# Graph-kernel layer with LayerNorm: one stationary operand moved, the banks of the preparation emptied by other engines, and three lists reordered

## The chip, the cores and the metric

One core of a Trainium2 chip runs the whole kernel. The metric is device time in microseconds, the median of several executions. The engines are called as in the profile: PE (TensorE), DVE (VectorE), ACT (ScalarE), POOL (GpSimd) and SP (SyncE, which here only issues DMAs).

## The reference, cut to what matters

`x` is 32 x 256 x 512, `adj` a 256 x 256 mask of zeros and ones. All is float32.

```python
z_l = einsum('bnd,ed->bne', x, W_lang);  z_g = einsum('bnd,ed->bne', x, W_grav)
v   = einsum('bnd,ed->bne', x, W_V)
zn  = z_l / max(norm(z_l), EPS)
A_l = max(zn zn^T, 0) * not_eye
d2  = max(sq + sq^T - 2 z_g z_g^T, 0)          # sq = row sums of z_g^2
A_g = exp(-d2 / (2 sigma^2)) * not_eye
K_l = A_l*adj / max(rowsum(A_l*adj), EPS);  K_g = the same of A_g
K   = w_l K_l + (1 - w_l) K_g                  # w_l = sigmoid(gate_logit)
x   = layernorm(x + (K v) W_O^T)
```

## The kernel before

**Products.** Every float32 matrix that PE multiplies is kept as two fp32r parts, hi (ACT rounds a bank or a tile into it) and lo (DVE subtracts hi from the source), and a product of two matrices is a sum of part products, hi·hi, hi·lo and lo·hi. The weights are first folded: M_g = W_g^T W_g for g = L (lang) and G (grav), so that x M x^T gives both Gram matrices, and WVO = W_V^T W_O^T. M is symmetric. What is computed for x is P = M x^T and then X = x P, of which X plus its own transpose is the Gram matrix. `m_hi` and `m_lo` are the parts of M, `md_hi` is the diagonal blocks of M with their lower triangle halved and joined with lo, and `wvo_hi`, `wvo_lo` the parts of WVO.

**The loop.** The 32 samples go in 16 pairs. The list of PE for pair p, with q = p - 1, is: eight projections `project(p, k)`, k = 0 to 7 (j = k mod 4 is the block of 128 output features, g = k div 4 is L or G), each into one bank of 128x512; `value(0, 0)` (12 products); four tiles of X, `x_tile` (8 products each); `value(0, 1)`; two tiles K times v of the sample 0 of pair q, `k_times_v` (6 products each); `value(1, 0)`; `value(1, 1)`; two tiles K times v of sample 1. Each product has a stationary operand of 128x128 and a moving one of 128x512. A projection has four products with x hi and four with x lo, one for each block i of 128 input features. That is 64 + 48 + 32 + 24 = 168 products a pair.

**Banks.** Banks 0 to 3 are used in turn by the preparation units, the projections and the values: a projection k waits until DVE has made the lo part of projection k - 4 (`proj_ready`). Banks 4 and 5 hold X, 6 and 7 K times v. ACT turns a projection's bank into `p_hi`, then DVE makes `p_lo`; the X tiles need all eight of them.

**Other engines.** Per pair DVE also transposes x blocks (`turn`), makes `hT_lo` (`turn_lo`), transposes X as it comes back from HBM (`turn_x`), adds (`gram`), masks, sums, scales (`gauss_masked`, `inverse_masked`, `cosine_masked`, `row_factors`, `kernel_sum`), transposes K (`turn_k`), splits it (`kt_lo_part`), and adds x (`residual`). `inverse_masked` needs the row of inverse norms in all partitions: `store_r` writes it to HBM and `spread_r` brings it back into `r_row`. X and K are rearranged through HBM as well (`spill_x` and `return_x`, `spill_k` and `return_k`). `load_x` brings x for the residual into `x_nat`, and `store` writes the output. All of these DMAs are issued by SP, in one list by hand. Every engine's list is written out by hand as the function `pair`, with semaphore waits between engines; there is no scheduler. Pairs 0, 1, 14 and 15 are unrolled, pairs 2 to 13 are a loop over two. The last pair has its own list on each engine, in which X and K are turned by PE.

**Preparation.** 22 units u = 0 to 21 go through banks u mod 4: UPPER L 0 to 3, UPPER G 0, then MIRROR L 1, WO_TURN 0, UPPER G 1, MIRROR L 2, WO_TURN 1, UPPER G 2, MIRROR L 3, WO_TURN 2 and 3, UPPER G 3, and MIRROR G 1, WVO 0, MIRROR G 2, WVO 1, MIRROR G 3, WVO 2, WVO 3. UPPER g i makes a block row of M_g from its diagonal block on (12 products of 512, 384, 256 or 128 columns), MIRROR copies the blocks below the diagonal by transposes of `m_hi`, WO_TURN transposes W_O, WVO makes a block row of WVO (12 products of 512). `m_lo` is corrected by the ratio of the diagonals: `diagonals` collects these, `scales` makes four small factors and `scaled_rest` passes over four slices of `m_lo`; then POOL makes `md_hi` of them (`join_triangles`, semaphore `m_ready`). DVE empties the MIRROR banks, POOL makes both parts of W_V.

## Time and profile before

| | us |
|---|---|
| median of 3 runs | 666.3 (665.96 to 666.48) |
| the profiled execution, device time | 666.75 |
| its span in the trace | 665.0 |
| PE busy | 650.5 (98%) |
| DVE busy | 538.7 (81%) |
| ACT busy | 376.6 (57%) |
| POOL busy | 138.8 (21%) |

The trace covers one execution; 1.75 us of its device time lie outside the span. Times below count from the span's start. A PE product is listed with its full latency of 389 ns, but products follow one another at a shorter distance; the distance is read from the starts. PEclk is the granted clock, 1.00 being 2.4 GHz. A duration of DVE or ACT in a list is some 0.08 us longer than the distance to the next operation behind it.

### The profile page before, as it was taken

How to read it: one execution, taken by the hardware profiler on the slowest of the kernel's cores; microseconds unless marked ns; L12 is line 12 of the kernel's file. 1: busy time of each engine (PE TensorE's matmuls, PEld its weight loads, DVE VectorE, ACT ScalarE, POOL GpSimd, SP SyncE). 2: the span in 40 equal slices, each digit the busy share in tenths (PEclk: the TensorE clock that was granted, in tenths of full speed). 3: DMA queues.
4: the chain of work that ended last, by engine and by line, in shares of the span. 5: the costliest groups of instructions: out<-in, count | busy, mean ns of one | idle time of the engine just before them, and what ended most of it. 6: DMA issues, size and time to landing. Idle time of an engine off the chain costs nothing.

```text
span 665.0 us, 10795 instructions
## 1 busy us (share of the span) xinstructions
PE 650.5 (98%) x2892; PEld 538.4 (81%) x2892; DVE 538.7 (81%) x1438; ACT 376.6 (57%) x697; POOL 138.8 (21%) x292
## 2 busy tenths in 40 slices
PE   8799999999999999999999999999999999999995
PEld 7688888888888888888888888888888888888784
DVE  6974878888788888888888798878888888887886
ACT  4242544665557465665656466555746566563746
POOL 4620202130311112131221213031111213121123
PEclk9799999999999999999999999999999999999999
DMA  9120627456483847658483765748384665647423
GB/s 300 33 83 13 190 66 231 118 185 164 149 231 116 235 107 225 137 159 205 151 231 88 235 147 173 174 143 235 110 235 112 212 147 161 175 147 221 156 79 126
DMA packets 141509, 106.48 MB, mean 160 GB/s; under 512 B 40112, under 2 KB 115632, under 8 KB 141488
## 3 DMA queue, kind: packets, MB, share of 16 engines
q1 hardware_dynamic: 140768, 104.40, 55.8%
q0 software_dynamic: 288, 1.05, 0.5%
q10 hardware_dynamic: 432, 0.79, 0.3%
q8 instruction: 9, 0.15, 0.1%
q14 instruction: 12, 0.10, 0.1%
HBM read 65.80 MB, written 40.40 MB: 160 GB/s over the span
## 4 chain that ended last, share of the span: by engine, by line
PE 92%; DVE 4%; DMA 1%; ACT 1%; issue 0%; SPq 0%; POOL 0%; POOLq 0%; DVEq 0%; ACTq 0%
PE bank L1370 57%; PE bank L1435 16%; PE bank L1439 16%; PE bank L1392 1%; DMA x_nat<-in_x 1%; DVE m_lo L968 1%; DVE x_nat L947 1%; DMA xs<-in_L_gnn_W_lang 0%; PE bank L1402 0%; DVE p_lo L1016 0%; DVE work L1071 0%; PE bank L1478 0%; DVE m_lo L935 0%; DVE work L1105 0%; ACT y L778 0%
## 5 line engine op out<-in xcount | busy, mean ns | idle before, releaser
L1439 PE MATMUL bank<-hT_lo,m_hi 128*128 128x512 f32 x512 | 136.8, 389 | 0.0
L718 ACT ACTIVATE p_hi<-bank,m_scale 128x512 fp32r<-128x512 f32 x128 | 87.6, 686 | 74.3 <-PE bank L1439 73.3
L1439 PEld LDWEIGHTS bank<-hT_lo,m_hi 128*128 128x128 f32 x512 | 96.1, 188 | 20.0
L1016 DVE SCALAR_TENSOR_TENSOR p_lo<-bank,m_scale,p_hi 128x512 fp32r<-128x512 f32 x128 | 92.7, 742 | 17.8 <-ACT p_hi L718 17.5
L722 ACT CAST v_hi<-bank 128x512 fp32r<-128x512 f32 x60 | 34.9, 581 | 118.7 <-PE bank L1370 118.6
L1370 PE MATMUL bank<-p_hi,hT_hi 128*128 128x512 f32 x256 | 99.7, 389 | 0.6 <-DVE p_lo L1016 0.6
L1370 PE MATMUL bank<-wvo_hi,hT_hi 128*128 128x512 f32 x256 | 99.9, 390 | 0.0
L1370 PE MATMUL bank<-wvo_lo,hT_hi 128*128 128x512 f32 x256 | 99.6, 389 | 0.0
L1370 PE MATMUL bank<-wvo_hi,hT_lo 128*128 128x512 f32 x256 | 99.6, 389 | 0.0
L1370 PE MATMUL bank<-p_lo,hT_hi 128*128 128x512 f32 x256 | 99.6, 389 | 0.0
L1154 DVE SCALAR_TENSOR_TENSOR y<-bank,x_nat 128x512 f32<-128x512 f32 x60 | 40.3, 688 | 37.7 <-DMA x_nat<-in_x 22.4
L598 POOL TENSOR_TENSOR rnorm<-norm,minus_half 128x2 f32<-128x2 f32 x32 | 35.2, 1101 | 135.0 <-DVE norm L1041 135.0
L733 ACT COPY xs<-bank 128x512 f32<-128x512 f32 x64 | 37.4, 584 | 42.7 <-PE bank L1370 42.6
L1435 PE MATMUL bank<-hT_hi,m_lo 128*128 128x512 f32 x192 | 59.2, 390 | 0.3 <-DVE p_lo L1016 0.3
L1435 PE MATMUL bank<-hT_hi,m_hi 128*128 128x512 f32 x192 | 59.1, 389 | 0.0
L1370 PEld LDWEIGHTS bank<-p_hi,hT_hi 128*128 128x128 f32 x256 | 48.1, 188 | 11.0 <-DVE p_lo L1016 1.0
L1370 PEld LDWEIGHTS bank<-wvo_hi,hT_hi 128*128 128x128 f32 x256 | 48.1, 188 | 10.2 <-DVE p_lo L1016 0.3
L1370 PEld LDWEIGHTS bank<-wvo_hi,hT_lo 128*128 128x128 f32 x256 | 48.0, 188 | 10.0
L1370 PEld LDWEIGHTS bank<-p_lo,hT_hi 128*128 128x128 f32 x256 | 48.0, 188 | 9.9
L1370 PEld LDWEIGHTS bank<-wvo_lo,hT_hi 128*128 128x128 f32 x256 | 48.1, 188 | 9.9
L1435 PE MATMUL bank<-hT_hi,md_hi 128*128 128x512 f32 x128 | 49.8, 389 | 0.0
L623 POOL TENSOR_TENSOR msq<-row_sq,one_by_d 128x2 f32<-128x2 f32 x30 | 5.9, 198 | 197.8 <-ACT junk_a L770 197.7
(155 smaller groups left out, 1250.6 us busy)
## 6 DMA issues: line engine op xcount, KB each, us to landing
x_blk<-in_x SPq DMA_DIRECT2D x128, 128.0 KB, 3.3
x_spill<-xs SPq DMA_DIRECT2D x30, 512.0 KB, 2.9
xq<-x_spill SPq DMA_DIRECT2D x120, 128.0 KB, 3.1
x_nat<-in_x SPq DMA_DIRECT2D x30, 512.0 KB, 4.6
out_y<-y SPq DMA_DIRECT2D x30, 512.0 KB, 3.3
k_spill<-work SPq DMA_DIRECT2D x30, 256.0 KB, 2.2
...
```

The costliest lines, as they stand in the source:

```text
L598: nc.gpsimd.tensor_tensor(rnorm[:, b, 0:NT], norm2[:, b], minus_half[:], ALU.pow).then_inc(pool_steps, 1)
L718: nc.scalar.activation(p_hi[:, :, j, g, :], src[:].rearrange("p (b n) -> p b n", b=2), ACT.Copy, scale=m_scale[:, g, j:j + 1]).then_inc(pr ...
L722: nc.scalar.copy(last_v(m_hi, b, t) if is_last(p) else v_hi[:, b, t], src[:]).then_inc(proj_hi, 1)
L733: nc.scalar.copy(dst, src).then_inc(x_saved, 1)
L947: nc.vector.tensor_tensor_reduce(out=x_nat[:, g, s, a:e], in0=tile[:, g, i, a:e].bitcast(F32), in1=ident[:], scale=sign, scalar=0.0, op0=A ...
L968: nc.vector.scalar_tensor_tensor(out=m_lo[:, g, i, i * P:], in0=m_hi[:, g, i, i * P:].bitcast(F32), scalar=steps_of[g][:, 4, i:i + 1], in1 ...
L1016: nc.vector.scalar_tensor_tensor(out=p_lo[:, :, j, g, :], in0=src[:].rearrange("p (b n) -> p b n", b=2), scalar=m_scale[:, g, j:j + 1], in ...
L1154: nc.vector.scalar_tensor_tensor(out=y[:, b, t], in0=kv_bank[t][:], scalar=1.0, in1=x_nat[:, b, t], op0=ALU.mult, op1=ALU.add, accum_out=r ...
L1370: last = pe.matmul(dst, lhsT, rhs, start=(n == 0), stop=(n == len(steps) - 1))
L1392: last = pe.matmul(dst[:, cols], lhsT, rhs, start=(n == 0), stop=(n == len(steps) - 1))
L1435: pe.matmul(pbank(k)[:], stationary, hi[i], start=(i == 0), stop=False)
L1439: last = pe.matmul(pbank(k)[:], m_hi[:, g, i, c], lo[i], start=False, stop=(i == DT - 1))
```

## The change

The lo part of the first 128 features of x (i = 0) is no longer a moving operand in the projections with j > 0. In its place each X tile gets a ninth product, with that lo part stationary and `p_hi` of block 0 moving. The lo products of the projections with j = 0 stay, with `md_hi` for the diagonal block. A pair has 58 + 48 + 36 + 24 = 166 products.

```diff
-                for i in range(DT):
-                    last = pe.matmul(pbank(k)[:], m_hi[:, g, i, c], lo[i], start=False, stop=(i == DT - 1))
+                for i in range(1 if j > 0 else 0, DT):
+                    last = pe.matmul(pbank(k)[:], md_hi[:, g, 0] if i == 0 else m_hi[:, g, i, c], lo[i], start=False,
+                                     stop=(i == DT - 1))
...
                     steps += [(lhsT, part[:, b, i].rearrange("p g n -> p (g n)")) for part in (p_hi, p_lo)]
+                steps.append((hT_lo[parity][:, 0, b, t * P:(t + 1) * P], p_hi[:, b, 0].rearrange("p g n -> p (g n)")))
```

On PE the fourth to the sixth row below are projection k = 1 of a pair (bank3), L1439 and L1464 being the products with x lo.

```order
L1439 MATMUL bank2<-hT_lo0,m_hi 128x512 x4
L1435 MATMUL bank3<-hT_hi0,m_lo 128x512
L1435 MATMUL bank3<-hT_hi0,md_hi 128x512
L1435 MATMUL bank3<-hT_hi0,m_hi 128x512 x2
L1439 MATMUL bank3<-hT_lo0,m_hi 128x512 x4
```

```order
L1464 MATMUL bank2<-hT_lo0,m_hi 128x512 x3
L1459 MATMUL bank3<-hT_hi0,m_lo 128x512
L1459 MATMUL bank3<-hT_hi0,md_hi 128x512
L1459 MATMUL bank3<-hT_hi0,m_hi 128x512 x2
L1464 MATMUL bank3<-hT_lo0,m_hi 128x512 x3
```

The upper piece is before, the lower one after: the last row has lost one product, as it has in the six projections with j > 0.

**Preparation.** ACT, not DVE, empties the MIRROR banks, in the order of the units, and a new function says which semaphore frees a bank. ACT also makes the hi part of W_V, POOL only the lo part. The first half of `join_triangles` no longer waits for `scaled_rest`. The wait of DVE for `m_ready` moves from ahead of pair 0 to its first `diagonal`.

```diff
+            def value_weight_hi(k):
+                act.wait_ge(w_loaded[2][k // 2], 16)
+                nc.scalar.copy(by_feature(w_parts[2][0][:, k]), in_order(raw[2][:, k])).then_inc(v_hi_ready, 1)
...
+                act.wait_ge(prep_done, u + 1)
                 if kind == MIRROR:
-                    return
-                act.wait_ge(prep_done, u + 1)
+                    nc.scalar.copy(m_hi[:, g, i, 0:i * P], src[:, 0:i * P]).then_inc(mirrored, 1)
+                    return
...
+            def emptied(u):
+                if prep_units[u][0] == MIRROR:
+                    pe.wait_ge(mirrored, mirrors_upto(u))
+                else:
+                    pe.wait_ge(prep_lo, upto_unit(u))
...
-                    pe.wait_ge(prep_lo, u - 3)
+                    emptied(u - 4)
...
-                if kind == UPPER and g == L:
-                    diagonals(L, i)
-                    if i == DT - 1:
-                        scales(L)
-                        scaled_rest(L)
-                if kind == UPPER and g == G and i < DT - 1:
-                    diagonals(G, i)
+                if kind == UPPER and (g, i) != (G, DT - 1):
+                    diagonals(g, i)
                 if u in SPLIT_AT:
                     turn_lo(0, 0, SPLIT_AT[u])
-                if u in TURN_AT:
-                    turn(0, TURN_AT[u])
-                if (kind, g, i) == (MIRROR, G, 1):
+                if (kind, g, i) == (UPPER, G, DT - 1):
+                    turn(0, 0)
                     diagonals(G, DT - 1)
+                    scales(L)
+                    scaled_rest(L)
+                if (kind, i) == (WVO, 0):
+                    turn(0, 1)
+                if (kind, i) == (WVO, 1):
                     scales(G)
-                if (kind, g, i) == (WVO, None, 1):
+                if (kind, i) == (WVO, 2):
                     scaled_rest(G)
```

On DVE, behind the diagonals of UPPER L 3, before. L957 to L963 are `scales(L)`, L968 is `scaled_rest(L)`, L935 empties the bank of UPPER G 0.

```order
L957 TENSOR_SCALAR junk_d<-junk_d 128x4
L959 RECIPROCAL junk_d<-junk_d 128x4
L961 TENSOR_TENSOR junk_d<-junk_d 128x4
L963 TENSOR_SCALAR m_scale<-junk_d 128x4
L968 SCALAR_TENSOR_TENSOR m_lo<-m_hi,junk_d,m_lo 128x512
L968 SCALAR_TENSOR_TENSOR m_lo<-m_hi,junk_d,m_lo 128x384
L968 SCALAR_TENSOR_TENSOR m_lo<-m_hi,junk_d,m_lo 128x256
L968 SCALAR_TENSOR_TENSOR m_lo<-m_hi,junk_d,m_lo 128x128
L935 TENSOR_TENSOR m_lo<-bank0,m_hi 128x512
```

The same place after. L951 is L935 of before, L955 empties the bank of WO_TURN 0, L963 is `diagonals`.

```order
L951 TENSOR_TENSOR m_lo<-bank0,m_hi 128x512
L963 ISA x_nat,junk_d<-m_hi,ident 128x128
L963 ISA junk_d 128x1
L963 ISA x_nat,junk_d<-m_lo,ident 128x128
L963 ISA junk_d 128x1
L955 TENSOR_TENSOR hT_lo1<-bank2,hT_hi1 128x512
L951 TENSOR_TENSOR m_lo<-bank3,m_hi 128x384
```

The four passes and the four small operations ahead of them have moved 25 rows down, behind UPPER G 3 and the first `turn`.

**Loop.** The lists of DVE, ACT and SP of a pair are reordered; no operation is added or removed there.

```diff
 # DVE
+                gauss_masked(q, 0)
                 gram(q, 0, L)
-                gauss_masked(q, 0)
                 proj_lo_part(p, 0)
                 cosine_masked(q, 0)
                 row_factors(q, 0)
                 proj_lo_part(p, 1)
+                turn_x(q, 1)
                 proj_lo_part(p, 2)
-                turn_x(q, 1)
                 proj_lo_part(p, 3)
-                kernel_sum(q, 0)
                 gram(q, 1, G)
                 proj_lo_part(p, 4)
-                inverse_masked(q, 1)
-                gram(q, 1, L)
+                kernel_sum(q, 0)
                 proj_lo_part(p, 5)
                 proj_lo_part(p, 6)
                 proj_lo_part(p, 7)
+                inverse_masked(q, 1)
                 gauss_masked(q, 1)
+                gram(q, 1, L)
...
+                kt_lo_part(q, 0)
                 turn_r(p, 0)
-                kt_lo_part(q, 0)
                 diagonal(p, 1)
                 turn_lo(p + 1, 1 - parity, 1)
-                residual(q, 0, 0)
                 turn(p + 2, 0)
                 proj_lo_part(p, 8)
                 turn_r(p, 1)
+                residual(q, 0, 0)
                 turn_k(q, 1)
+                residual(q, 0, 1)
+                kt_lo_part(q, 1)
                 proj_lo_part(p, 9)
-                kt_lo_part(q, 1)
-                residual(q, 0, 1)
                 turn_x(p, 0)
                 gram(p, 0, G)
                 residual(q, 1, 0)
+                inverse_masked(p, 0)
                 residual(q, 1, 1)
                 proj_lo_part(p, 10)
-                inverse_masked(p, 0)
                 proj_lo_part(p, 11)
 # SP
                 return_k(q, 0)
+                load_x(q, 0)
+                spill_k(q, 1)
                 store(q - 1, 0)
-                spill_k(q, 1)
-                load_x(q, 0)
+                load_x(q, 1)
                 spill_x(p, 0)
                 return_k(q, 1)
                 store_r(p, 0)
                 return_x(p, 0)
+                store(q - 1, 1)
                 spill_x(p, 1)
-                store(q - 1, 1)
-                load_x(q, 1)
+                store_r(p, 1)
                 spread_r(p, 0)
-                store_r(p, 1)
```

On ACT `squares(q - 1, 0)` goes ahead of the first `proj_hi_part`, `squares(q - 1, 1)` and `gauss(q, 1)` go from behind the eighth to behind the fifth, both `normalise` and `gauss(p, 0)` go a few places ahead, and `save_x(p, 1, 0)` goes behind `kt_hi_part(q, 0)`. The lists of the last pair are as they were.

On DVE, from the x lo split of a pair (L914, L932) to the values, before and then after. L1154 and L1172 are `residual`, L1024 and L1039 the values' lo parts, L1137 and L1155 `turn_k`, L1144 and L1162 `kt_lo_part`.

```order
L1154 SCALAR_TENSOR_TENSOR y,row_sum<-bank6,x_nat 128x512
L906 STREAM_TRANSPOSE hT_raw<-x_blk 128x1024
L1024 TENSOR_TENSOR v_lo<-bank2,v_hi 128x512
L1049 STREAM_TRANSPOSE rnormT<-rnorm 128x32
L1137 STREAM_TRANSPOSE work<-work 128x8x2x32
L1024 TENSOR_TENSOR v_lo<-bank3,v_hi 128x512
L1144 TENSOR_TENSOR kt_lo<-work,kt_hi 128x512
L1154 SCALAR_TENSOR_TENSOR y,row_sum<-bank7,x_nat 128x512
```

```order
L924 STREAM_TRANSPOSE hT_raw<-x_blk 128x1024
L1039 TENSOR_TENSOR v_lo<-bank2,v_hi 128x512
L1067 STREAM_TRANSPOSE rnormT<-rnorm 128x32
L1172 SCALAR_TENSOR_TENSOR y,row_sum<-bank6,x_nat 128x512
L1155 STREAM_TRANSPOSE work<-work 128x8x2x32
L1172 SCALAR_TENSOR_TENSOR y,row_sum<-bank7,x_nat 128x512
L1162 TENSOR_TENSOR kt_lo<-work,kt_hi 128x512
L1039 TENSOR_TENSOR v_lo<-bank3,v_hi 128x512
```

Both residuals of sample 0 now stand around `turn_k` of sample 1, and the second `v_lo` has gone behind the split of that K.

## Rows read from the trace of the kernel before

**Rows 1.** page, busy time of the engines
```profile
PE 650.5 (98%) x2892; PEld 538.4 (81%) x2892; DVE 538.7 (81%) x1438; ACT 376.6 (57%) x697; POOL 138.8 (21%) x292
```

**Rows 2.** busy time by stretch: preparation, and one pair of the loop
```profile
core 0: us, PE busy (x) PEld busy (x) DVE busy (x) ACT busy (x) POOL busy (x), PEclk, DMA share, GB/s
19.27:32.17 12.90, 8.12 (x43) 7.55 (x43) 11.67 (x26) 2.71 (x6) 8.44 (x11) 0.74 0.01 3
228.67:266.75 38.08, 38.08 (x169) 31.53 (x169) 31.80 (x85) 22.68 (x42) 7.33 (x16) 1.00 0.63 173
```

**Rows 3.** who waited, PE over the whole run: us, times, longest
```profile
PE bank L1397 <- DVE m_lo L935: 3.9, 1, 3.9
...
PE bank L1402 <- DVE m_hi L931: 0.9, 1, 0.9
PE bank L1370 <- DVE p_lo L1016: 0.6, 1, 0.6
```

**Rows 4.** page, costliest groups: us, mean ns, idle before
```profile
L1439 PE MATMUL bank<-hT_lo,m_hi 128*128 128x512 f32 x512 | 136.8, 389 | 0.0
...
L1370 PE MATMUL bank<-wvo_hi,hT_lo 128*128 128x512 f32 x256 | 99.6, 389 | 0.0
```

**Rows 5.** timeline of PE, preparation: start us, us, what
```profile
11.10 0.28 PE L1392 MATMUL bank<-p_hi 128*128 128x256 f32 x1
...
13.82 0.44 PE L1392 MATMUL bank<-p_hi 128*128 128x512 f32 x1
...
32.17 0.47 PE L1370 MATMUL bank<-hT_hi,v_hi 128*128 128x512 f32 x1
...
43.77 0.39 PE L1435 MATMUL bank<-hT_hi,md_hi 128*128 128x512 f32 x1
```

**Rows 6.** timeline of DVE, preparation
```profile
14.81 1.06 DVE L947 CUSTOM_DVE_ANT_0 x_nat<-m_hi,ident 128x128 f32<-128x128 f32 x1
...
18.38 4.33 DVE L968 SCALAR_TENSOR_TENSOR m_lo<-m_hi,junk_d,m_lo 128x512 fp32r<-128x512 f32 x4
...
33.91 0.27 DVE L947 CUSTOM_DVE_ANT_0 x_nat<-m_hi,ident 128x128 f32<-128x128 f32 x1
...
34.44 0.17 DVE L957 TENSOR_SCALAR junk_d<-junk_d 128x4 f32<-128x4 f32 x1
...
42.47 1.93 DVE L968 SCALAR_TENSOR_TENSOR m_lo<-m_hi,junk_d,m_lo 128x512 fp32r<-128x512 f32 x4
...
44.78 1.28 DVE L939 TENSOR_TENSOR wvo_lo<-bank,wvo_hi 128x512 fp32r<-128x512 f32 x2
45.98 1.23 DVE L906 STREAM_TRANSPOSE hT_raw<-x_blk 128x1024 f32<-128x1024 f32 x1
```

**Rows 7.** timeline of ACT, preparation
```profile
47.25 1.05 ACT L673 CAST hT_hi<-hT_raw 128x1024 fp32r<-128x1024 f32 x1 [2.50 <-DVE hT_raw L906]
```

**Rows 8.** timeline of POOL, preparation
```profile
20.71 1.45 POOL L560 TENSOR_TENSOR v_lo<-xq,v_hi 128x512 fp32r<-128x512 f32 x1
...
44.49 1.01 POOL L574 TENSOR_TENSOR junk_a<-m_hi,junk_d 128x384 f32<-128x384 f32 x1 [15.93 <-DVE m_lo L968]
...
47.39 1.29 POOL L578 TENSOR_TENSOR md_hi<-junk_a 128x512 fp32r<-128x512 f32 x1
```

**Rows 9.** timeline of DVE, a pair of the loop
```profile
236.98 1.30 DVE L1060 STREAM_TRANSPOSE work<-xq 128x512 f32<-128x512 f32 x2 [0.62 <-DMA xq<-x_spill]
...
244.16 0.75 DVE L1016 SCALAR_TENSOR_TENSOR p_lo<-bank,m_scale,p_hi 128x512 fp32r<-128x512 f32 x1 [0.68 <-ACT p_hi L718]
```

**Rows 10.** timeline of SP, the same pair
```profile
262.25 1.16 SPq L444 DMA_DIRECT2D r_row<-r_spill  x1
```

**Rows 11.** tile r_row, two pairs of the loop
```profile
DMA to landing us min/median/max: 3.9/4.8/5.3
```

**Rows 12.** timeline of PE, the last pair
```profile
609.53 0.39 PE L1435 MATMUL bank<-hT_hi,md_hi 128*128 128x512 f32 x1
...
628.32 0.50 PE L1370 MATMUL bank<-p_hi,hT_hi 128*128 128x512 f32 x1 [0.57 <-DVE p_lo L1016]
```

More of the change, by code:

```diff
@@ L319, in gnn_resnorm @@
         PREP = len(prep_units)
-        TURN_AT = {prep_units.index((UPPER, G, DT - 1)): 0, prep_units.index((MIRROR, G, 2)): 1}
         SPLIT_AT = {prep_units.index((WVO, None, 0)): 0, prep_units.index((WVO, None, 1)): 1}
         def prepared(kind, g, i):
-            return prep_units.index((kind, g, i)) + 1
+            return upto_unit(prep_units.index((kind, g, i)))
         def of_projection(k):
@@ L335, in upto_unit, with mirrors_upto, mirror_of @@
             return sum(kind != MIRROR for kind, _, _ in prep_units[:u + 1])
+        def mirrors_upto(u):
+            return sum(kind == MIRROR for kind, _, _ in prep_units[:u + 1])
+        def mirror_of(g, i):
+            return mirrors_upto(prep_units.index((MIRROR, g, i)))
         def live(p):
@@ L571, in join_triangles @@
                     pool.wait_ge(m_ready[L], 1)
+                pool.wait_ge(prep_lo, prepared(UPPER, g, DT - 1))
                 for part, (tile, mask) in enumerate(((m_hi, lower_half), (m_lo, upper_strict))):
+                    if part == 1:
+                        pool.wait_ge(m_scaled[g], DT)
                     many, one = diagonal_blocks(tile, g)
@@ L703, in _ @@
                     weight_hi(G, 2 + i)
+                if (kind, g, i) == (UPPER, L, DT - 1) or (kind, i) == (WO_TURN, 0):
+                    for k in range(2):
+                        value_weight_hi(k if kind == UPPER else 2 + k)
             act.wait_ge(scal_loaded, 32)
@@ L783, in pair @@
                 q = p - 1
+                squares(q - 1, 0)
                 proj_hi_part(p, 0)
-                squares(q - 1, 0)
                 proj_hi_part(p, 1)
                 proj_hi_part(p, 2)
+                normalise(q - 1, 0)
+                gauss_scaled(q, 0)
                 proj_hi_part(p, 3)
-                gauss_scaled(q, 0)
-                normalise(q - 1, 0)
                 proj_hi_part(p, 4)
+                squares(q - 1, 1)
+                gauss(q, 1)
                 proj_hi_part(p, 5)
@@ L1028, in diagonal @@
                 dve.wait_ge(x_saved, upto(p, 4, 2 * b + 2))
+                if type(p) is int and p == 0 and b == 0:
+                    for g in (L, G):
+                        dve.wait_ge(m_ready[g], 1)
                 for g, sign in ((G, -1.0), (L, 1.0)):
@@ L1428, in project @@
                 else:
-                    pe.wait_ge(prep_lo, PREP - 3 + k)
+                    emptied(PREP - 4 + k)
                 hi = [hT_hi[parity][:, i].rearrange("p b n -> p (b n)") for i in range(DT)]
```

22 lines of the change are left out of this document (8 added, 14 removed).

## The prediction

> **What bounds the kernel now.** I read the busy times first: PE is busy for 650.5 of 665.0 us, DVE for 538.7 [rows 1]. Then one pair of the loop: in 38.08 us PE is busy for all of it, at a granted clock of 1.00, and DVE for 31.8 [rows 2]. Then the list of who waited: PE waited 3.9 and 0.9 us in the preparation and 0.6 in the last pair, and no row of it falls in the loop [rows 3]. So the loop costs what its products cost: 38.08 / 168 = 0.2267 us a product. A product with x lo as stationary operand already stands among the values and shows the same mean of 389 ns as one with x lo moving [rows 4], so I price the ninth product of an X tile at 0.2267 too. Last the preparation, where PE is busy for only 8.12 of the 12.90 us from 19.27 to 32.17, at a mean clock of 0.74 [rows 2]: it sat idle first and then ran partly at 1.2 GHz.
>
> **Products.** Six projections lose one each, four X tiles gain one: 2 x 0.2267 = 0.453 us a pair. For pairs 0 to 14 that is 15 x 0.453 = 6.8 us, if no wait comes instead. The last pair is another matter. Its X tiles start at 628.32, 18.79 us after its first product at 609.53, and they wait for the last `p_lo` [rows 12]; 76 products before them need only 17.23. DVE's list there is unchanged and was full, so six products fewer let PE arrive earlier and wait longer. I let the tiles start 0.2 us sooner, because DVE comes a little earlier out of pair 14 (the x for its residual is loaded sooner), and then they last 4 x 0.2267 = 0.9 longer: the last pair gets 0.7 slower, between 0.9 slower and, if DVE had slack after all, 0.45 faster.
>
> **Does the loop stay full?** Counting from a pair's first product, projection k = 7 now ends at 58 x 0.2267 = 13.15 and the X tiles start after 12 products more, at 15.87 (before 17.23). Each `p_lo` costs ACT and DVE one operation. The last one began at 244.16, 15.4 into the pair, after 0.68 of waiting for ACT [rows 9], and took 0.75. With everything 1.36 earlier it would end at 14.8, a margin of 1.1. That asks that DVE has 1.36 us less to do by then. One `inverse_masked` and one `gram` (0.6 each) move behind the last `p_lo`, and another `inverse_masked` moves ahead of `residual(q, 1, 1)`: 1.8 us are taken out, so the new list fits. Earlier banks are looser: `p_lo` of k = 2 must be ready at 44 x 0.2267 = 9.97. The risk in that place is `turn_x(q, 1)`, now ahead of it. Before, it waited for its DMA until 236.98, 8.3 into the pair [rows 9]. `load_x` and `store` have left the stretch of SP's list just ahead of the eight block loads and `return_x`, and I work with 2 us less: DVE's list reaches `turn_x` at about 6.1, the data come at about 6.2, and `p_lo` of k = 2 is ready at 8.1, 1.9 us early. In the second half K x v of sample 0 starts at 118 x 0.2267 = 26.75 (before 27.2) and needs `kt_lo`, which follows the second X tile: that tile ends 0.9 us earlier than before, so the margin grows. Each residual moved behind `proj_lo_part(p, 8)` has until the K x v of sample 1 at 34.9, some 3 us. ACT is busy for 22.7 of 38.08 and hides its moves; POOL and SP likewise. I take no new wait, and keep 0.3 a pair as the bound upward.
>
> **Preparation.** PE waited 3.9 us for the bank of UPPER G 0, which DVE emptied only after `scaled_rest(L)`, 4.33 us for four passes from 18.38 on [rows 3, 6]. The same four passes take 1.93 us at 42.47, when POOL is idle [rows 6, 8]. In the new order PE needs from 19.27: UPPER G 2 and G 3, which at full clock took UPPER L 2 and L 3 from 11.10 to 13.82, 2.72 us [rows 5]; and 18 transposes at no more than 2.72 / 24 = 0.11 each, 2.0. That gives WVO 0 at 24.0 instead of 32.17. DVE must empty seven banks meanwhile (0.6 us or less each: two of 512 columns take 1.28 [rows 6]) and take three pairs of diagonals of 0.4: 5.1 us from 17.5 on, where ACT has rounded UPPER G 0, so 22.6. But POOL, which worked on W_V until 22.2 [rows 8], still makes its lo part, and beside it one diagonal operation took 1.06 instead of 0.27 [rows 6]. Two pairs can lose 1 us each: 24.6. I take WVO 0 at 24.6, 7.6 us earlier; the bounds are 24.0 and 26. The four WVO units take 43.77 - 32.17 = 11.6 us as before [rows 5], so pair 0 starts at 36.2.
>
> What is late next is DVE, which brings its backlog along. From 24.6 its list is: four full passes over 1024 columns (two `turn`, two `turn_lo`, 1.15 each [rows 6]) with 1.6 us of waiting for ACT in between, since ACT rounds x (1.05 [rows 7]) ahead of WVO 1; four WVO banks at 0.6; `scales` twice at 0.8 (four operations of 0.17 that wait for one another [rows 6]); `scaled_rest` twice at 1.9; UPPER G 3 and diagonals 0.6; and `turn(1, 0)` 1.15. Sum 15.8, so 40.4. Then ACT rounds that x, 1.0, and makes the first `p_hi`, 0.65 like a bank on DVE, and DVE `p_lo`, 0.7: 42.8. Projection k = 4 needs that bank and would start at 36.2 + 29 x 0.2267 = 42.8. It also needs `md_hi` of G: `scaled_rest(G)` ends at 38.6, and POOL needs 2.9 of the 4.2 us that it took from 44.49 to 48.7, as half of the masks is now done ahead [rows 8]: 41.5. So the first bank just fits; I charge 0.1, with 1.5 as a bound.
>
> **The port.** The rows show four passes slowed from 1.93 to 4.33 us beside POOL [rows 6]. The Trainium skill, "SBUF — State Buffer", section "Who interferes with whom", says that a VectorE instruction with two SBUF inputs and a GpSimd instruction that reads SBUF exclude each other for a whole instruction. By that rule the move of `scaled_rest(L)` away from POOL's W_V work is worth 2.4 us more than a mere reordering; that agrees with the rows, and by the same rule the first three pairs of diagonals stay exposed, which is the 2 us that I charge.
>
> **The sum.** 666.75 for the profiled execution, less 7.6 - 0.1 = 7.5, less 6.8, plus 0.7, is 653.15. The median of the runs is 0.45 lower than that execution: 652.7 us.
>
> **Rivals.**
> - B: `return_x` of sample 1 is as late as before. `turn_x(q, 1)` then starts at 8.3, and `p_lo` of k = 2 is ready at 8.3 + 1.2 + 0.66 = 10.2 for a bank wanted at 9.97: 0.25 us a pair, 14 pairs, 3.5 us, 656.2. For it: the landing was last there before. Against: the queue ahead is shorter.
> - C: the preparation gives back half. DVE's backlog holds up pair 0, or the passes meet POOL again at 4.33 instead of 1.93: 2.4 to 3.8 us, 655 to 656.5. For it: the margin at k = 4 is zero.
> - D, slower: `spread_r(p, 0)` now stands behind `store_r(p, 1)`, and `inverse_masked(p, 0)`, which waits for its row, stands ahead of `residual(q, 1, 1)` and both last `v_lo`. Before, it was issued at 262.25, 33.6 into the pair [rows 10], and a row lands 3.9 to 5.3 us after issue [rows 11]. Projection k = 2 of the next pair starts at 3.40 and needs the first of these `v_lo`, three operations of 0.6 behind the row: the row has to be there at 1.5. Issued at 32.4 of 37.63 it lands between -1.3 and 0.1. Each us beyond 1.5 is 1 us a pair; from 2.5 on, the gain of 0.45 a pair and that of the preparation (0.5 when spread over 14 pairs) are gone; at 3.0 it is 14 x 1.5 - 13.6 = 7 us slower, 674. Against it: that asks for a landing 7.7 us after issue, and the longest seen is 5.3.
> - E: two products fewer are not worth their distance, or the ninth costs more, since each X tile ends on another pair of operands. With nothing gained a pair: 652.7 + 6.8 = 659.5. Against it: equal means [rows 4]. The Trainium skill, "TensorE: Matmul & The Clock Gate", section "Back-to-back issue gap", gives 131 ns as sustained distance for 512 columns. By that the 32 products would be worth 4.2 us instead of 7.25 and the time 655.7; this case's 226.7 ns over 168 products speaks against it.
>
> **Chances.** Forecast 0.68, B 0.12, C 0.11, E 0.05, D 0.04. The range from 651.0 (WVO 0 at 24.0, last pair not slower) to 657.0 holds the forecast with its bounds, B and C; E and D are out. Within 0.2% (1.3 us), about what a measurement of this kernel can tell from no change, lies hardly anything: 0.01. Faster 0.94, slower 0.05, for D and like waits that I have not seen.
>
> **What would show it.** A pair of the loop should last 37.63 us with PE busy throughout; 37.9 and a wait of PE for `p_lo` at k = 2 is B; a wait for `v_lo` is D; 38.08 without a wait is E. WVO 0 should start at 24.6 and pair 0 at 36.2, at a granted clock of 1.00 from 19 us on; a PE wait at k = 4 of pair 0 is C. In the last pair the wait ahead of the X tiles should grow, and one at k = 7 with it. The forecast is wrong if PE waits in the loop at all, or if the preparation ends later than 38.

## The result, and the profile after

The changed kernel takes 657.6 us (median of 4 runs, 656.85 to 658.0) against 666.4 for the kernel before: a ratio of 0.9868, interval 0.9851 to 0.9885. It is faster, as forecast, but by 8.8 us (1.3%) and not by 13.6; 657.6 lies 0.6 above the range. The profiled execution took 658.0, its span 656.3, so it is compared with the 653.15 of the sum: 4.85 us are missing.

I cut both traces at the first product of each pair. The forecast column is the prediction's sum, term by term.

| stretch, us | before | forecast | after |
|---|---|---|---|
| start to pair 0 | 43.77 | 36.2 | 36.95 |
| pair 0 | 32.64 | 32.3 | 33.88 |
| pair 1 | 38.08 | 37.63 | 39.60 |
| pairs 2 to 14 (13 of them) | 495.04 | 489.2 | 489.15 |
| last pair, to the end | 55.5 | 56.2 | 56.7 |

The loop is as forecast to the hundredth. Everything that is missing lies outside it: 0.75 ahead of pair 0, 1.6 in pair 0, 1.97 in pair 1, 0.5 in the last pair.

The busy line of the page after (compare [rows 1]: PE is busy for 8.8 us less, 3.0 of them in the preparation, of which no part runs at the lower clock any more, and 5.9 from pair 0 on; it is still busy for 98%):
```profile
PE 641.7 (98%) x2860; PEld 529.5 (81%) x2860; DVE 536.7 (82%) x1432; ACT 381.2 (58%) x707; POOL 140.8 (21%) x288
```

Busy time by stretch, after: the second half of the preparation, pair 0, pair 1, and pair 2 (compare [rows 2]):
```profile
core 0: us, PE busy (x) PEld busy (x) DVE busy (x) ACT busy (x) POOL busy (x), PEclk, DMA share, GB/s
19.30:36.95 17.65, 16.79 (x97) 14.30 (x96) 14.81 (x33) 7.93 (x16) 10.41 (x12) 1.00 0.23 64
110.43:148.06 37.63, 37.63 (x168) 31.16 (x166) 32.04 (x85) 22.73 (x42) 7.71 (x16) 1.00 0.63 174
36.95:70.83 33.88, 32.47 (x143) 26.57 (x142) 22.85 (x57) 14.31 (x25) 7.32 (x10) 1.00 0.21 65
70.83:110.43 39.60, 38.30 (x167) 31.00 (x166) 31.62 (x83) 17.71 (x31) 4.18 (x7) 1.00 0.56 155
```
Pair 2 is full: 37.63 of 37.63. Pairs 0 and 1 have holes of 1.41 and 1.30. They lose more than that (1.7 and 1.97 against 32.19 and 37.63 without a wait), since a hole is counted from the end of the 389 ns of the product ahead of it, 0.16 us behind the moment at which the next one could have started, and the products behind it follow more slowly at first.

Who PE waited for, after (us in total, times, longest; compare [rows 3]):
```profile
PE bank L1459 <- DVE p_lo L1031: 3.8, 3, 1.4
PE bank L1437 <- POOL kt_hi L543: 1.4, 1, 1.4
PE bank L1426 <- DVE hT_lo L955: 0.8, 1, 0.8
```
The 3.9 us for `m_lo` are gone; the 1.4 for `kt_hi` stand at the very start of both kernels. L1459 is the first half of a projection; its three waits for `p_lo` are one in pair 0, one in pair 1, one in the last pair. In the timeline of PE they stand here (start, duration, operation, and in brackets the wait ahead of it):
```profile
25.35 0.47 PE L1387 MATMUL bank<-hT_hi,v_hi 128*128 128x512 f32 x1
...
45.10 0.47 PE L1459 MATMUL bank<-hT_hi,md_hi 128*128 128x512 f32 x1 [1.41 <-DVE p_lo L1031]
...
74.67 0.74 PE L1459 MATMUL bank<-hT_hi,m_lo 128*128 128x512 f32 x2 [0.28 <-DVE v_lo L1039]
...
82.60 0.74 PE L1459 MATMUL bank<-hT_hi,m_lo 128*128 128x512 f32 x2 [1.02 <-DVE p_lo L1031]
...
612.65 0.98 PE L1459 MATMUL bank<-hT_hi,m_lo 128*128 128x512 f32 x3 [1.33 <-DVE p_lo L1031]
...
618.25 0.50 PE L1387 MATMUL bank<-p_hi,hT_hi 128*128 128x512 f32 x1 [0.61 <-DVE p_lo L1031]
```
The first row is WVO 0, the one at 45.10 projection k = 4 of pair 0, at 82.60 k = 6 of pair 1, the last two k = 7 and the X tiles of the last pair.

### The profile page after: what moved, and what is told of

It reads as the page before. It is cut to its first block, busy times and chain, and to the rows that moved or that the text cites. A ratio compares the mean times of both kernels' runs of the same rounds, so it can differ in the third digit from the quotient of the medians.

```text
span 656.3 us, 10731 instructions
## 1 busy us (share of the span) xinstructions
PE 641.7 (98%) x2860; PEld 529.5 (81%) x2860; DVE 536.7 (82%) x1432; ACT 381.2 (58%) x707; POOL 140.8 (21%) x288
## 3 DMA queue, kind: packets, MB, share of 16 engines
q0 software_dynamic: 288, 1.05, 0.5%
## 4 chain that ended last, share of the span: by engine, by line
PE 86%; DVE 8%; ACT 2%; DMA 1%; SPq 1%; issue 1%; POOL 0%; POOLq 0%; DVEq 0%
PE bank L1387 56%; PE bank L1459 15%; PE bank L1464 12%; PE bank L1416 2%; SPq L410 1%; DVE hT_raw L924 1%; DMA xq<-x_spill 1%; DVE p_lo L1031 1%; DVE hT_lo L932 1%; DVE m_lo L984 1%; DMA xs<-in_L_gnn_W_lang 0%; DVE work L1078 0%; DVE wvo_lo L955 0%; DVE x_nat L963 0%; DVE x_blk L1238 0%
## 5 line engine op out<-in xcount | busy, mean ns | idle before, releaser
L1464 PE MATMUL bank<-hT_lo,m_hi 128*128 128x512 f32 x384 | 107.9, 389 | 0.0
L736 ACT ACTIVATE p_hi<-bank,m_scale 128x512 fp32r<-128x512 f32 x128 | 84.9, 684 | 36.9 <-PE bank L1464 36.8
L1464 PEld LDWEIGHTS bank<-hT_lo,m_hi 128*128 128x128 f32 x384 | 72.1, 188 | 15.1
L1039 DVE TENSOR_TENSOR v_lo<-bank,v_hi 128x512 fp32r<-128x512 f32 x60 | 39.8, 684 | 28.1 <-ACT v_hi L740 28.1
L1459 PE MATMUL bank<-hT_hi,m_lo 128*128 128x512 f32 x192 | 59.5, 391 | 2.6 <-DVE p_lo L1031 2.4
L1459 PE MATMUL bank<-hT_hi,m_hi 128*128 128x512 f32 x192 | 59.1, 389 | 0.0
L1459 PE MATMUL bank<-hT_hi,md_hi 128*128 128x512 f32 x128 | 49.9, 390 | 1.4 <-DVE p_lo L1031 1.4
L1053 DVE CUSTOM_DVE_ANT_0 junk_d<-xs,ident 128x128 f32<-128x128 f32 x128 | 29.7, 288 | 23.4 <-ACT xs L751 23.2
```

Source lines behind the costliest of these rows:

```text
L736: nc.scalar.activation(p_hi[:, :, j, g, :], src[:].rearrange("p (b n) -> p b n", b=2), ACT.Copy, scale=m_scale[:, g, j:j + 1]).then_inc(pr ...
L1039: nc.vector.tensor_tensor(dst, src[:], hi.bitcast(F32), ALU.subtract).then_inc(proj_ready, 1)
L1053: ins = nc.vector.tensor_tensor_reduce(out=junk_d[:, g, t].rearrange("p (j a) -> p j a", a=BLK), in0=block, in1=ident[:].rearrange("p (j a ...
L1459: pe.matmul(pbank(k)[:], stationary, hi[i], start=(i == 0), stop=False)
L1464: last = pe.matmul(pbank(k)[:], md_hi[:, g, 0] if i == 0 else m_hi[:, g, i, c], lo[i], start=False, stop=(i == DT - 1))
```

## Experiments: the parts by themselves

Four kernels, timed with the kernel before on one chip (666.2).

**166 products alone** (e1), in the kernel before:

> The kernel before with the 166 products alone: preparation and all three lists as before. Theory 1 (a product is worth 0.2267 us, and the old lists leave PE full with 166 too): pairs of 37.63 us, pair 0 starting at 43.77, the last pair some 0.7 to 1.2 longer, 660 to 661 us, and no wait of PE in pairs 1 to 14. Rival (the old lists don't fit into projections that are 1.36 us shorter): PE waits for p_lo in each pair, 0.2 to 0.5 us, pairs of 37.85 to 38.1, 663 to 667 us.

660.05 us, ratio 0.9906 (0.9884 to 0.9928). All pairs from 1 to 14 take 37.63, pair 0 32.19; none of them waits. Pair 0 starts at 42.57 and not at 43.77: the preparation of this execution began 0.55 us sooner and ran 0.65 shorter, with no edit in it. The products are worth 6.2 us (the forecast's terms for them and the last pair were 6.8 less 0.7), and the old lists feed them.

**The new preparation alone** (e2; 168 products, old lists):

> The kernel before with the new preparation alone: 168 products, old lists. Theory 1: pair 0 starts at about 37 (36.95 in the changed kernel) instead of 43.77, projection k = 4 of pair 0 still waits (1 to 1.6 us, some 0.3 less than in the changed kernel since it is wanted later), pair 1 starts without a further wait: 661 to 662 us. Rival (the wait of pair 1 comes from the shorter preparation, not from the new lists): 663 to 664 us.

661.33 us, ratio 0.9924 (0.9902 to 0.9946): 4.9 us. Pair 0 starts at 37.10, and already here it loses 0.95 us at k = 4. Pair 1 takes 38.08, without a wait.

**The new lists alone** (e3):

> The kernel before with the new lists of DVE, ACT and SP alone: 168 products, old preparation. Theory 1: pairs of the loop stay at 38.08 us, and pair 1 gets the wait that it has in the changed kernel, behind inverse_masked of pair 0 and turn_x: 0.5 to 1.9 us slower than before, 667 to 668. Rival (the lists cost nothing anywhere): 666.4.

666.06 us, ratio 1.000 (0.999 to 1.001). Pair 1 loses 0.30, less than the 0.5 that theory 1 asked for at least, and the time doesn't show it.

**The changed kernel with the old lists** (e4):

> The changed kernel with the old lists of DVE, ACT and SP. Theory 1 (the new lists aren't needed, and cost 1.9 us in pair 1): pairs of 37.63 us, no wait in pair 1 beyond 0.3, 655.5 to 656.5 us. Rival (they are needed for 166 products): a wait in each pair, 660 us or more. Measured for the changed kernel: 657.6.

655.74 us, ratio 0.9839 (0.9817 to 0.9862). Pairs 2 to 14 take 37.63, pair 1 38.60. Theory 1 had allowed pair 1 a wait of 0.3; it loses 0.97. Products and preparation bring 10.5 together. The changed kernel takes 1.85 more than this one (1.65 between the two profiled executions), and 1.0 of it stands in pair 1 (39.60 against 38.60). Another 0.66 is only that the preparation of this execution began that much sooner: UPPER L 2 starts at 10.57 and not at 11.23. Over the traces shown here that start varies from 10.34 to 11.33. So what the new lists cost is read from pair 1 of the traces, and not from the times, whose intervals overlap; and pair 1 itself varies: it took 39.31 in f4 below, whose edit doesn't touch it.

## Experiments: the wait in pair 0

Ahead of that wait stand, on DVE and ACT of the changed kernel:
```profile
30.36 1.65 DVE L932 TENSOR_TENSOR hT_lo<-hT_raw,hT_hi 128x1024 fp32r<-128x1024 f32 x1
...
35.58 1.59 DVE L932 TENSOR_TENSOR hT_lo<-hT_raw,hT_hi 128x1024 fp32r<-128x1024 f32 x1
...
40.50 0.68 DVE L955 TENSOR_TENSOR wvo_lo<-bank,wvo_hi 128x512 fp32r<-128x512 f32 x1
41.10 1.23 DVE L924 STREAM_TRANSPOSE hT_raw<-x_blk 128x1024 f32<-128x1024 f32 x1
...
42.29 1.19 DVE L1016 TENSOR_TENSOR scal<-scal 128x1 f32<-128x1 f32 x1
...
44.20 2.73 DVE L1031 SCALAR_TENSOR_TENSOR p_lo<-bank,m_scale,p_hi 128x512 fp32r<-128x512 f32 x4
```
```profile
42.36 1.06 ACT L682 CAST hT_hi<-hT_raw 128x1024 fp32r<-128x1024 f32 x1 [4.43 <-DVE hT_raw L924]
43.32 2.42 ACT L736 ACTIVATE p_hi<-bank,m_scale 128x512 fp32r<-128x512 f32 x4
```
The first bank of projections is full at 38.8, but ACT stands idle for 4.43 us until DVE has transposed x of pair 1. Nobody needs that x in the first half of pair 0. So I moved them (f1):
```diff
-            turn(1, 0)        # DVE, with the eight operations on scal; turn_hi(1, 1, 0) on ACT likewise
...
                 proj_lo_part(p, 3)
+                if type(p) is int and p == 0:
+                    turn(1, 0)
+                    scal_factors()
```

> The changed kernel, with three things moved from the end of the preparation into pair 0, behind the fourth bank of projections: DVE's turn(1, 0), the eight small operations on scal, and ACT's turn_hi(1, 1, 0). Theory 1 (DVE's and ACT's backlog at the end of the preparation is what holds up projection k = 4 of pair 0): the first p_hi no longer waits for the rounding of x (1.06 us from 42.36) and the small operations, p_lo of k = 0 is ready at about 42 and not at 44.9, pair 0 takes 32.2 us and not 33.88, the time falls by 1.6 us to about 656.0. Rival 2 (md_hi of G is as late: POOL ends it at 43.47 and k = 4 would start at 43.5; or scaled_rest(G) itself is the backlog): 0.5 to 1.5 us of the wait stay, with another releaser, and the time falls by less than 1 us. Rival 3: the moved work is late inside pair 0 and DVE stands in the way of p_lo there: pair 0 stays above 33.

655.13 us, ratio 0.9836 (0.982 to 0.9853). Pair 0 takes 32.32: 1.56 us of the wait are gone, theory 1 holds. ACT makes the first `p_hi` at 38.42 and DVE its `p_lo` at 40.45. `md_hi` of G is there just in time (POOL makes it at 41.52, in 1.29, and k = 4 starts at 42.9), and k = 4 follows k = 3 without a gap. The time fell by 2.46, more than the 1.56: the preparation of this execution began 0.64 sooner, and pair 1 and the last pair, in which the edit changes nothing, were 0.3 and 0.4 shorter. So here too the pair in the trace is the measure.

## Experiments: the wait in pair 1

Two things in pair 1 had changed places on DVE, and both wait for a DMA. DVE and SP, changed kernel:
```profile
73.32 0.69 DVE L1113 TENSOR_TENSOR work<-r_row,adj_off 128x512 f32<-128x512 f32 x1 [3.01 <-DMA r_row<-r_spill]
73.93 1.28 DVE L1039 TENSOR_TENSOR v_lo<-bank,v_hi 128x512 fp32r<-128x512 f32 x2
...
80.61 1.31 DVE L1078 STREAM_TRANSPOSE work<-xq 128x512 f32<-128x512 f32 x2 [1.50 <-DMA xq<-x_spill]
81.84 1.37 DVE L1031 SCALAR_TENSOR_TENSOR p_lo<-bank,m_scale,p_hi 128x512 fp32r<-128x512 f32 x2
```
```profile
68.90 0.44 SPq L453 DMA_DIRECT2D r_row<-r_spill  x1
69.38 5.11 SPq L410 DMA_DIRECT2D x_blk<-in_x  x8
74.53 1.93 SPq L423 DMA_DIRECT2D xq<-x_spill  x4
```
L1113 is `inverse_masked(0, 0)`, rival D's place; L1078 is `turn_x(0, 1)`, rival B's; L410 the block loads, L423 `return_x(0, 1)`. Three edits, each for one pair alone, tell them apart.

**The mask back in its old place** (f2; `inverse_masked(0, 0)` behind `proj_lo_part(p, 10)`):

> The changed kernel, but in pair 0 alone inverse_masked(0, 0) stands behind the third v_lo, as in the kernel before. DVE waited 3.01 us there for r_row. Theory 1 (the 2 us lost in pair 1 have two causes: this wait, which delays v_lo and pushes all behind it, and return_x of sample 1, whose data reach DVE at 80.6, 9.8 into the pair): with the first cause gone the PE wait for v_lo at k = 2 (0.28) goes, the wait at k = 6 for p_lo stays at about 1.0, pair 1 takes 38.9 to 39.3 and not 39.60. Rival 2 (the wait for r_row is the whole cause, as my rival D had it): pair 1 takes 37.7, the time falls by 1.9 us. Rival 3 (it has no part, the transfer is the whole cause): pair 1 stays at 39.6.

657.31 us; pair 1 takes 39.67. DVE waits 0.57 for the row and then 2.29 for `xq`: the same data, waited for longer. Rival 3 holds: the row has no part in it.

**`return_x(0, 1)` ahead of the block loads** (f5):
```diff
+                if type(p) is int and p == 1:
+                    return_x(q, 1)
+                    spread_r(q, 1)
                 load_blocks(p + 1, 1)
                 load_blocks(p + 2, 0)
```

> The changed kernel, but in pair 1 alone SP issues return_x(0, 1) and spread_r(0, 1) ahead of the eight block loads (5.1 us of issuing) and not behind them. Theory 1: in pair 1 the data of turn_x(0, 1) land some 5 us sooner, DVE does not wait for xq, the wait of PE for p_lo goes, and only the wait for r_row (0.3 to 1 us) stays: pair 1 takes 37.9 to 38.7, the time falls by 1 to 1.7 us. Rival 2 (the wait for r_row is the whole cause): pair 1 stays at 39.5. Rival 3: return_x waits for spill_x of pair 0 and stands then in front of the loads: x of pair 2 comes late, a new wait appears in pair 1 or 2, nothing gained.

655.68 us, ratio 0.9846 (0.9829 to 0.9862). Pair 1 is full:
```profile
68.84 1.91 SPq L423 DMA_DIRECT2D xq<-x_spill  x4
70.79 0.45 SPq L453 DMA_DIRECT2D r_row<-r_spill  x1
71.29 5.12 SPq L410 DMA_DIRECT2D x_blk<-in_x  x8
```
```profile
70.29:107.92 37.63, 37.63 (x168) 31.17 (x166) 31.54 (x83) 17.70 (x31) 4.18 (x7) 1.00 0.57 162
```
This is better than theory 1, which left a part to the row: DVE still waits 2.22 for it, and PE never notices. The whole 1.97 us were the late `return_x`. (`spread_r(0, 1)` moved with it, but DVE reaches that row only 16.7 us into pair 1 and didn't wait for it in the changed kernel.)

**`turn_x(0, 1)` behind the third `p_lo`, in pair 1 alone** (f3):
```diff
                 proj_lo_part(p, 1)
-                turn_x(q, 1)
+                if not (type(p) is int and p == 1):
+                    turn_x(q, 1)
                 proj_lo_part(p, 2)
+                if type(p) is int and p == 1:
+                    turn_x(q, 1)
```

> The changed kernel, but in pair 1 alone turn_x(0, 1) stands again behind the third p_lo, as in the kernel before. The transfer is as late as in the changed kernel (data at about 80.0 to 80.6). Theory 1 (the place of turn_x ahead of the third p_lo turns the late transfer into a stall, as rival B of the prediction had it for the loop): that p_lo is made before the wait, PE loses only what it lost with the old lists, pair 1 takes 38.6 us, the time falls by 1.0 us to about 656.5. Rival 2 (the place is of no account, DVE is held up for the same time either way and a later p_lo is late instead): pair 1 stays at 39.3 to 39.7.

655.85 us, ratio 0.9838 (0.9822 to 0.9855); pair 1 takes 38.02, better than the 38.6 expected. The data come at 80.19, as late as ever (9.8 us into the pair), but only 0.39 us is lost. So the transfer is late wherever `turn_x` stands (in e4 DVE waited 2.39 us for it and PE lost 0.97), and its new place makes 1.6 of the 2 us.

Why in pair 1 only? The prediction took 2 us off the transfer because `load_x` and `store` had left the stretch of SP's list ahead of the block loads. In the loop that came true. Before, SP issued `return_x` of sample 1 2.5 us into a pair (the second row, pair from 266.75); the first row is pair 1, 3.4 us after its start at 76.41:
```profile
79.85 1.93 SPq L414 DMA_DIRECT2D xq<-x_spill  x4
...
269.28 1.85 SPq L414 DMA_DIRECT2D xq<-x_spill  x4
```
After, in a pair of the loop that begins at 223.31, SP issues it at the start:
```profile
219.29 3.90 SPq L410 DMA_DIRECT2D x_blk<-in_x  x8
223.24 1.92 SPq L423 DMA_DIRECT2D xq<-x_spill  x4
```
```profile
229.73 1.31 DVE L1078 STREAM_TRANSPOSE work<-xq 128x512 f32<-128x512 f32 x2 [0.23 <-DMA xq<-x_spill]
```
But pair 0 has no pair ahead of it, so its list holds neither a `load_x` nor a `store`, and no gain could come from moving them: in pair 1 `return_x` is issued 3.7 us after the start (74.53, pair from 70.83), no earlier than before. In the loop DVE starts `turn_x` 6.4 us into the pair; in pair 1 it was 9.8, with the third `p_lo` wanted at 9.97. Before, the data came at 8.9 in pair 1, behind the third `p_lo` on DVE's list. That they come another 0.9 us later now goes with the new preparation more than with the lists: DVE started on them at 8.4 in e1 (both old; nothing was lost), 8.9 in e3 (new lists), 9.4 in e4 (new preparation) and 9.8 with both. Why is open; in h2 below SP issued `return_x` 2.5 us into pair 1, and the data still came at 10.0.

## Experiments: the last pair

The lists (f4) of DVE and ACT there up to the X tiles, in the order of the loop: all eight `proj_lo_part` ahead of `turn_k(q, 0)` and of `gauss_masked`, `cosine_masked`, `row_factors` and `kernel_sum` of sample 1.

> The changed kernel, with the lists of DVE and ACT in the last pair up to the X tiles in the order that the loop now has. Theory 1 (the list of the last pair, not the amount of work of DVE, sets the start of its X tiles): PE's waits of 1.33 and 0.61 us at k = 7 and ahead of the X tiles go, and these start 15.9 to 16.9 us into the pair and not 18.67. What stood ahead of the last p_lo (0.7 for turn_k, 2.4 for gauss_masked, cosine_masked, row_factors and kernel_sum of sample 1) must be done behind it, so part of this comes back in front of the diagonals: the time falls by 1 to 2.5 us. Rival 2 (the work of DVE is the limit for the whole pair): the X tiles start sooner but the tail grows by as much, the time stays within 0.5 us. Rival 3: K times v of sample 0 of pair 14 or the last Gram matrices now wait longer, and the time is above 658.5.

656.29 us, ratio 0.985 (0.9834 to 0.9867). The X tiles start 15.87 us into the pair, which is the 70 products ahead of them at 0.2267, and both waits are gone. But from these tiles to the end it is 40.0 us and not 38.0. PE now waits further on:
```profile
637.03 0.66 PE L1515 MATMUL bank<-ident,hT_raw 128*128 128x128 f32 x4 [0.71 <-DVE hT_raw L1277]
641.67 0.66 PE L1515 MATMUL bank<-ident,hT_raw 128*128 128x128 f32 x4 [1.22 <-DVE hT_raw L1277]
```
L1515 turns the last K, which DVE makes in `last_kernel_sum`. Of 2.8 us, 0.8 stay: the list set the start of the tiles, but the tail behind them has a chain of its own through DVE, which takes back the rest.

## Experiments: the preparation

**`scales(L)` and `scaled_rest(L)` in their old place** (h1), the rest as changed:

> The changed kernel, but scales(L) and scaled_rest(L) stand again behind the diagonals of UPPER L 3, where POOL works on W_V beside them. Theory 1 (this move carries half or more of the gain of the preparation, by the slowed passes): the four passes take 4.3 us and not 1.93, PE waits some 4 us for the bank of UPPER G 0, a part of which DVE gives back later since these 1.9 us are done; pair 0 starts at 39 to 41 and not at 36.9, the time is 2 to 4 us above the changed kernel. Rival 2 (the passes are not slowed now, since ACT makes half of W_V, and only the order counts): the passes take 1.9 to 2.5 us, pair 0 starts at 37 to 38. Rival 3 (the place is of no account, DVE has the same list in sum): within 0.5 us.

660.59 us, ratio 0.9921 (0.9901 to 0.994), 3.0 us above the changed kernel. DVE and POOL:
```profile
14.43 1.13 DVE L973 TENSOR_SCALAR junk_d<-junk_d 128x4 f32<-128x4 f32 x1
15.60 0.18 DVE L975 RECIPROCAL junk_d<-junk_d 128x4 f32<-128x4 f32 x1
15.81 0.99 DVE L977 TENSOR_TENSOR junk_d<-junk_d 128x4 f32<-128x4 f32 x1
16.83 0.17 DVE L979 TENSOR_SCALAR m_scale<-junk_d 128x4 f32<-128x4 f32 x1
16.91 3.96 DVE L984 SCALAR_TENSOR_TENSOR m_lo<-m_hi,junk_d,m_lo 128x512 fp32r<-128x512 f32 x4
```
```profile
14.13 2.64 POOL L567 TENSOR_TENSOR v_lo<-xq,v_hi 128x512 fp32r<-128x512 f32 x2 [6.37 <-ACT v_hi L692]
17.91 2.80 POOL L567 TENSOR_TENSOR v_lo<-xq,v_hi 128x512 fp32r<-128x512 f32 x2 [1.14 <-ACT v_hi L692]
```
The four passes take 3.96 us beside POOL, and 1.93 in the changed kernel; the two slow small operations ahead of them add 1.8. So POOL costs DVE 3.8 us in this place, and rival 2 is out. Behind them PE waits 2.84 for the bank of UPPER G 0, and then its clock falls. Busy time from the end of that wait to WVO 0, the column behind POOL being the granted clock:
```profile
21.52:29.89 8.37, 7.79 (x42) 7.54 (x43) 5.34 (x18) 2.98 (x6) 4.82 (x8) 0.59 0.01 3
```
0.59 is mostly the lower level, 1.2 GHz. From UPPER L 2 to WVO 0 it takes 19.55 us, against 14.12 in the changed kernel: 5.4 us, 2.6 of them more waiting and 2.8 the slower clock. Pair 0 starts at 41.51, half a microsecond above what theory 1 allowed. The time grows by only 3.0, since pair 0, later by that much, does not wait at k = 4 (32.18).

**The MIRROR banks emptied by DVE again** (h2):

> The changed kernel, but DVE and not ACT empties the six MIRROR banks (the sum of their columns is 6 x 256, some 0.4 us each, 2.4 us of DVE), at the place of the units in its list. Theory 1 (DVE is what PE waits for in this preparation, and each us of it counts): pair 0 starts 1.5 to 3 us later than in the changed kernel, the time is 1.5 to 3 us higher. Rival (ACT is as short of time there, so the change of engine gave nothing): within 0.5 us.

657.91 us, ratio 0.9873 (0.9857 to 0.989): 0.3 above the changed kernel, inside the intervals. From UPPER L 2 to WVO 0 it takes 14.79 us, 0.67 more. Theory 1 asked for 1.5 or more and is wrong: ACT's help with these banks is worth some half a microsecond, and the place of `scales(L)` and the four passes nearly all. The hi part of W_V on ACT and the earlier half of `join_triangles` were not tested by themselves.

## Experiments: the price of a product, and what the lists are worth

**Without the ninth product** (g2, g3), 162 a pair, with the new lists and with the old ones:

> The changed kernel without the ninth product of the X tiles (the term x lo of block 0 times p_hi of block 0 is left out): 162 products a pair. It prices the ninth product and shows how much room DVE, ACT and the transfers have. Theory 1 (PE sets the loop, a product is worth 0.2267 us wherever it stands): a pair of the loop takes 162 x 0.2267 = 36.72 us with PE busy throughout, the time falls by about 13 x 0.91 + some = 12 to 14 us to 644 to 646. Rival 2 (the lists of DVE or the transfers have less than 0.9 us of room): a pair takes 36.8 to 37.6, with a wait of PE that names who is late. Rival 3 (the ninth product costs more than the others, because another pair of operands is read): a pair takes less than 36.7.

> As g2_no_ninth (the ninth product of the X tiles left out, 162 products a pair), but with the old lists. With the new ones most pairs took 36.72 us. Theory 1 (the old lists have less room, and this is what the reordering is for): pairs take 36.9 to 37.6 us with waits of PE for p_lo or v_lo. Rival 2 (the old lists have the same room): 36.72 us here too, and the new lists buy nothing even at 162 products.

New lists: 643.9 us (one run), a shade below the 644 to 646 expected. The pairs take 36.72 except pair 1 (38.51), 3 (37.69) and 4 (37.08). Old lists: 642.8 us (one run), 36.72 except pair 1 (37.54) and pair 8 (36.80). A pair of each:
```profile
300.00:336.72 36.72, 36.72 (x164) 30.41 (x163) 31.58 (x85) 22.79 (x43) 7.77 (x16) 1.00 0.65 179
```
```profile
107.03:143.75 36.72, 36.72 (x163) 30.42 (x162) 31.14 (x83) 22.59 (x42) 7.54 (x16) 1.00 0.63 172
```
The ninth product costs (37.63 - 36.72) / 4 = 0.2275 us, as any other. With the old lists DVE and the transfers had at least 0.9 us of room in every pair from 2 on (pair 8 lost 0.08). With the new ones pairs 3 and 4 did not have it. In pair 3, which begins at 144.44 and loses 0.97, DVE waits in both of the places that rivals D and B named, for the row and then for `xq`:
```profile
145.93 0.69 DVE L1113 TENSOR_TENSOR work<-r_row,adj_off 128x512 f32<-128x512 f32 x1 [1.77 <-DMA r_row<-r_spill]
...
153.25 1.30 DVE L1078 STREAM_TRANSPOSE work<-xq 128x512 f32<-128x512 f32 x2 [0.79 <-DMA xq<-x_spill]
```
So at 162 products it is the new lists that have less room. Each is one trace of one run.

**The three edits together** (f1, f5 and f4; runs g1 and g4), on the changed kernel and on its version with the old lists:

> The changed kernel with the three edits together that worked alone: the work moved from the end of the preparation into pair 0, return_x(0, 1) and spread_r(0, 1) ahead of the block loads in pair 1, and the last pair's lists in the order of the loop. Theory 1 (three separate stalls, whose prices add): pair 0 takes 32.3 us, pair 1 37.63, the X tiles of the last pair start 15.9 into it; 657.59 - 2.46 - 1.91 - 1.30 is 651.9 if the measured gains add, of which some 0.6 us were preparations that happened to run shorter, so 651.9 to 652.6. Rival: they hide one another (with pair 0 shorter by 1.6 us return_x(0, 1) comes late again), and 1 us or more is missing: above 653.

> As g1_three_mended (new preparation, 166 products, the three edits), but with the lists of DVE, ACT and SP of the kernel before in the pairs 0 to 14. Theory 1 (at 166 products the new lists carry nothing in the loop): pairs of 37.63, the time within 0.6 us of the 652.65 of g1_three_mended. Rival (with pair 1's transfer mended the new lists still win something at the ends of the loop, in pair 1 or ahead of the last pair): 0.7 us or more above.

652.65 us with the new lists, ratio 0.9796 (0.978 to 0.9813), and 652.84 with the old ones, ratio 0.9791 (0.9775 to 0.9807). Pair 0 takes 32.32 and 32.27, pair 1 37.63 in both, the X tiles of the last pair start at 15.87. This is 5 us below the changed kernel and 14 below the kernel before; in its trace no wait of PE is left between the preparation and the last K. The stalls were separate: pair 0, pair 1 and the last pair give back 1.56, 1.97 and 1.2 us in one kernel, as they did alone or a little more. The order of the lists makes no difference that can be measured, at 166 products.

## Why the prediction was wrong, and where it was right

**The products were right.** 0.2267 us each, the same with x lo as stationary operand, no new wait in pairs 2 to 14; alone they bring 6.2 us. Rival E is out. The reordering of the lists that the prediction thought was needed for this was not: e1 and e4 have the same loop with the old lists.

**"The first bank just fits; I charge 0.1" was the first step that failed**, by 1.6 us. My sum of DVE's list ended at 40.4 with `turn(1, 0)`; that ended at 42.3. 0.75 is the later WVO 0, 0.8 are the two `turn_lo`, 1.65 and 1.59 us beside POOL where I had put 1.15, and 0.3 the first operation of `scales(G)`, 0.43 beside POOL and not 0.17. The operations on `scal` behind it, 1.7 us, I had not counted; they end at 44.1 and hold up the first `p_lo` a little more. I had charged the slow operations beside POOL ahead of WVO 0 and forgotten them behind it. Rival C named the mechanism. f1 shows what my sum did not ask: the work that was late need not stand there.

**"I work with 2 us less" was the second, true in the loop and not in pair 1.** In the loop it holds: the data come at about 6.4, forecast 6.2. In pair 1 they come at 9.8. The 2 us were the `load_x` and `store` that left SP's list ahead of the loads, and pair 0 has none of them. The move of `turn_x` ahead of the third `p_lo` turned the late transfer into 1.97 us; before, that `p_lo` stood ahead of it. Rival B had the mechanism and the place, but took its delay from the loop and spread it over 14 pairs. Rival D's place stopped DVE in pair 1 too, for 3.01 us, but f2 shows that this cost nothing.

**The preparation was right in kind and 0.75 too good.** WVO 0 came at 25.35, not at 24.6. Its time was set where the forecast put it, at the end of DVE's list. DVE and the weight load of WVO 0, changed kernel:
```profile
20.11 0.56 DVE L951 TENSOR_TENSOR m_lo<-bank,m_hi 128x384 fp32r<-128x384 f32 x1 [0.69 <-ACT m_hi L703]
...
20.71 0.79 DVE L963 CUSTOM_DVE_ANT_0 x_nat<-m_hi,ident 128x128 f32<-128x128 f32 x1
...
21.43 1.08 DVE L963 CUSTOM_DVE_ANT_0 x_nat<-m_lo,ident 128x128 f32<-128x128 f32 x1
...
23.92 1.28 DVE L955 TENSOR_TENSOR hT_lo<-bank,hT_hi 128x512 fp32r<-128x512 f32 x2
...
25.32 0.19 PEld L1387 LDWEIGHTS bank<-hT_hi,v_hi 128*128 128x128 f32 x1 [0.25 <-DVE hT_lo L955]
```
From 20.11 to 25.20, when the last part of W_O was ready, DVE has no pause. What the sum left out is the 0.69 ahead of it, in which DVE stood idle until ACT had rounded UPPER G 1. The work itself took 5.6 and not 5.1 us. Against that, only one pair of diagonals was slowed beside POOL (1.3 us; I had charged 2 for two pairs), its second half beside the first half of `join_triangles`, which the change itself had moved there. PE was held up by the same slow pair:
```profile
23.18 0.66 PE L1426 MATMUL bank<-ident,y 128*128 128x128 f32 x4 [0.77 <-DVE hT_lo L955]
```
It was through with the transposes and UPPER G 3 behind this row only 0.1 to 0.2 us before DVE, so (an estimate) a shorter list of DVE alone would have brought little more. The reason given for the gain, the four passes, holds: h1.

**The last pair lost 1.2 and not 0.7.** The tiles start 18.67 us into the pair (forecast 18.6), but the tail behind them grew by 1.3 and not by 0.9, 0.16 of it in a wait for K. A part of this is chance: with the same lists of the last pair the tail took 37.6 us in e1, f1 and h2, and 38.0 here. The reason given for the earlier start of the tiles, an `x` loaded sooner, is not borne out: with the old lists (e1) they start at 18.66 too.

**The range** was built from the rivals' sizes one at a time. B in one pair and C in half came together, 3.6 us, with two small misses of 1.3 on top.
